# A decoder kernel on one Trainium2 core: gate layer and matrix powers made one unrolled stage

## The reference

```
g  = sigmoid(x @ Wg.T + bg)                # gate layer
u  = x * g                                 # gated input
h_t = A_c h_(t-1) + B_c u_t,  y_t = C_c h_t + D_c u_t      # for each channel c
```

## Time and profile before

| | |
|---|---|
| median of 3 runs | 5916.88 us (5911.08 to 5918.68) |
| profiled execution | 5911.98 us, span 5910.1 us |
| mean granted TensorE clock | 0.839 |
| PE busy | 4607.9 us, 78% |
| DVE / ACT / POOL busy | 3770.6 / 1886.1 / 2643.7 us |
| DMA | 625.22 MB, mean 106 GB/s |

### The profile page before, as it was taken

The page is one execution under the profiler, slowest core; times in us unless marked ns, Lnnn a source line. Parts: engine busy times, 40 slices in busy tenths (PEclk is TensorE's granted clock), DMA queues, the critical chain, the costliest instruction groups (busy, mean ns, idle before and its releaser), DMA issues. The chain is left out here.

```text
span 5910.1 us, 44058 instructions
## 1 busy us (share of the span) xinstructions
PE 4607.9 (78%) x13049; PEld 2461.4 (42%) x13057; DVE 3770.6 (64%) x3977; ACT 1886.1 (32%) x2769; POOL 2643.7 (45%) x1515
## 2 busy tenths in 40 slices
PE   7799796563999970997882887777777869968887
PEld 3699775442444420443330333333333323434443
DVE  2233342656224668554884999999999977744555
ACT  1111111111223446112773444334443334413332
POOL 0344452220001224010887899999999963311110
PEclk9555798555999985999886999989999989979998
DMA  1100112212223669452445115114142124510000
GB/s 64 63 0 0 41 57 84 89 54 87 93 96 139 224 240 374 152 189 88 172 167 209 56 59 174 60 65 160 58 147 72 60 107 163 202 66 22 28 28 22
DMA packets 314169, 625.22 MB, mean 106 GB/s; under 512 B 34407, under 2 KB 101896, under 8 KB 301204
## 3 DMA queue, kind: packets, MB, share of 16 engines
q1 hardware_dynamic: 295956, 589.74, 28.4%
q10 hardware_dynamic: 18048, 33.56, 1.5%
HBM read 404.48 MB, written 218.73 MB: 105 GB/s over the span
## 5 line engine op out<-in xcount | busy, mean ns | idle before, releaser
L1945 PE MATMUL sc_yp<-sc_Z,sc_idn 128*128 128x512 f32 x2048 | 1079.5, 664 | 425.1 <-POOL sc_Z L1875 216.9
L1869 POOL TENSOR_TENSOR sc_X<-sc_Bm,sc_w 128x1024 f32<-128x1024 f32 x512 | 1188.6, 2353 | 13.3 <-issue 12.5
L1945 PEld LDWEIGHTS sc_yp<-sc_Z,sc_idn 128*128 128x128 f32 x2048 | 411.5, 210 | 1053.3 <-issue 650.0
L1891 ACT ACTIVATE sc_A<-sc_dt,keep_A 128x1024 f32<-128x1024 f32 x512 | 572.1, 1117 | 526.6 <-DVE sc_Z L1981 427.0
L1110 PE MATMUL ff_ps<-ffn_R 128*128 128x512 f32 x1536 | 667.6, 595 | 7.8 <-ACT ff_o L1146 6.7
L1130 PE MATMUL ff_ps<-ffn_downT,ffn_R 128*128 128x512 f32 x768 | 332.8, 596 | 193.0 <-DVE ffn_R L1303 193.0
L1981 DVE TENSOR_TENSOR sc_Z<-sc_A,sc_Cm 128x1024 f32<-128x1024 f32 x384 | 470.1, 1224 | 17.6 <-issue 4.4
L1976 DVE TENSOR_TENSOR_SCAN sc_A<-sc_A,sc_hc,sc_X 128x1024 f32<-128x1024 f32 x192 | 450.2, 2345 | 0.0
L1110 PEld LDWEIGHTS ff_ps<-ffn_R 128*128 128x128 f32 x1536 | 290.3, 190 | 379.6 <-issue 352.1
L1976 DVE TENSOR_TENSOR_SCAN sc_A<-sc_A,sc_X 128x1024 f32<-128x1024 f32 x192 | 438.2, 2282 | 14.8 <-POOL sc_X L1869 14.8
L1875 POOL TENSOR_TENSOR sc_Z<-sc_H,sc_Cm 128x1024 f32<-128x1024 f32 x128 | 300.1, 2344 | 149.8 <-DVE sc_H L1976 149.8
(11 more groups left out here) (348 smaller groups left out, 7509.1 us busy)
## 6 DMA issues: line engine op xcount, KB each, us to landing
sc_Bm<-d_xd SPq DMA_DIRECT2D x64, 512.0 KB, 12.2
sc_Cm<-d_xd SPq DMA_DIRECT2D x64, 512.0 KB, 14.5
ffn_gate_d<-ff_o SPq DMA_DIRECT2D x96, 256.0 KB, 2.3
ff_g<-ffn_gate_d SPq DMA_DIRECT2D x24, 1024.0 KB, 6.0
ffn_up_d<-ff_o SPq DMA_DIRECT2D x96, 256.0 KB, 6.2
ffn_g_d<-ff_z SPq DMA_DIRECT2D x24, 1024.0 KB, 6.4
ffn_R<-ffn_g_d SPq DMA_DIRECT2D x24, 1024.0 KB, 7.2
ffn_R<-ffn_up_d SPq DMA_DIRECT2D x24, 1024.0 KB, 9.4
```

Source lines behind the costliest of these rows:

```text
L1869: nc.gpsimd.tensor_tensor(X[:, k % RX], Bm[:, n], w[:, j % 2], ALU.mult).then_inc(db, 1)
L1891: nc.scalar.activation(A[:, k % 2], dt[:, j % 2], ACT.Exp, scale=keepA[:, n:n + 1]).then_inc(ex, 1)
L1945: last = nc.tensor.matmul(yp[:, e * TB:(e + 1) * TB], idn[:], Z[:, k % RZ, e * TB:(e + 1) * TB], start=(n == 0), stop=(n == NS - 1))
```

## The change

`gate_stage` and `powers_stage` become `gate_powers_stage`. All loops are unrolled; the order of work is one list `STEPS` of (round i, m, u), 160 of them. There are 32 gate tiles (8 blocks x 4 slices) of four matmuls, and five steps to a tile: in the first four of each five steps TensorE does one gate matmul ahead of the step's own. Sigmoids go behind each fifth step on ScalarE, products behind the eviction of each fifth step on VectorE. The sigmoid is written in place in PSUM. The h matmuls move from the end of a round to m = 6, from an own buffer `cbd` that GpSimd fills at m = 5. The B rows are now taken out by VectorE too. A and C come packed in one array, and m = 0 uses it directly. The two PSUM tiles of the powers share one bank for each unit. The store of `xg` stands at the end of SP's program.

```diff
-def powers_stage(nc, a_pk, b_pk, c_pk, dp_pk, e0, mask, ident, keep, hp_d):
+def gate_powers_stage(nc, x_t, wg_t, bg, xgp, ac_pk, b_pk, dp_pk, e0, mask, ident, keep, hp_d):
+    STEPS = [(i, m, u) for i in range(NI) for m in range(SQ) for u in range(NS)]
+    TILES = T // NT * KD
+    EVERY = len(STEPS) // TILES
+    HM = 6
...
+        pg = s.ps("pg", [P, KD, NT])
+        pp = s.ps("pp", [P, NS, 512])
...
         @block.sync
+            for t, v in ((acin, ac_pk), (bin_, b_pk), (msk, mask), (idn, ident), (e0s, e0), (dp, dp_pk)):
                 sp.dma_start(t[:], v).then_inc(cst, 16)
+            sp.dma_start(w[:], wg_t.rearrange("(k p) e -> p k e", p=P)).then_inc(w_in, 16)
+            sp.dma_start(bias[:], bg).then_inc(w_in, 16)
+            for nb in range(T // NT):
+                if nb >= 2:
+                    sp.wait_ge(prod, 1 + (nb - 1) * KD)
+                sp.dma_start(x[:, nb % 2], x_v[:, :, nb * NT:(nb + 1) * NT]).then_inc(x_in[nb % 2], 16)
...
             sp.wait_ge(h_te, 2)
             sp.dma_start(hp_d[:, TAU:2 * TAU]..., ht[:]...).then_inc(out_d, 16)
+            sp.wait_ge(prod, 1 + TILES)
+            for k in range(KD):
+                sp.dma_start(xgp...[k], xg[:, k]).then_inc(stored, 16)
             sp.wait_ge(out_d, 33)
+            sp.wait_ge(stored, 1 + 16 * KD)
...
         @block.gpsimd
+            for i, m, u in STEPS:
+                if m == 0:
+                    pool.wait_ge(t_bd[u], 1 + i * SQ)
+                    pool.wait_ge(sq[u], 1 + max(i * SQ - SQ + 4, 0))
+                    expand(nc.gpsimd, pbd[:, u], acin[:, groups(i, u), 0:16], msk[:]).then_inc(p_bd[u], 1)
+                else:
+                    pool.wait_ge(ev[u], evicted(i, m - 1))
+                    expand(nc.gpsimd, pbd[:, u], r2[:, u, :, 0:16], msk[:]).then_inc(p_bd[u], 1)
+                if m == HM - 1:
+                    pool.wait_ge(h_mm[u], 1 + i)
+                    expand(nc.gpsimd, cbd[:, u], r2[:, u, :, 16:32], msk[:]).then_inc(c_bd[u], 1)
...
         @block.tensor
+            def gate_part(r):
+                t, k = r // KD, r % KD
+                nb, e = t // KD, t % KD
+                if r == 0:
+                    pe.wait_ge(w_in, 33)
+                if t >= KD:
+                    pe.wait_ge(prod, 1 + t - KD + 1)
+                pe.wait_ge(x_in[nb % 2], 1 + nb // 2 * 16 + 16)
+                last = nc.tensor.matmul(pg[:, e], w[:, k, e * P:(e + 1) * P], x[:, nb % 2, k], start=(k == 0), stop=(k == KD - 1))
+                if k == KD - 1:
+                    last.then_inc(mm, 1)
+            for c, (i, m, u) in enumerate(STEPS):
+                n = 2 ** m if m < 4 else 0
+                if c % EVERY < KD:
+                    gate_part(c // EVERY * KD + c % EVERY)
+                pe.wait_ge(t_bd[u], 1 + i * SQ + m + 1)
+                if m:
+                    pe.wait_ge(ev[u], evicted(i, m - 1))
...
+                if m == HM:
                     pe.wait_ge(c_bd[u], 1 + i + 1)
                     for g in range(GB):
+                        last = nc.tensor.matmul(ps1[:, u, g, 8:9], cbd[:, u, g], r1[:, u, g, 15:16], start=True, stop=True)
                     last.then_inc(h_mm[u], 1)
...
         @block.scalar
+            for c, (i, m, u) in enumerate(STEPS):
...
+                if c % EVERY == EVERY - 1:
+                    t = c // EVERY
+                    act.wait_ge(mm, 1 + t + 1)
+                    nc.scalar.activation(pg[:, t % KD], pg[:, t % KD], ACT.Sigmoid, bias=bias[:, t % KD:t % KD + 1]).then_inc(gated, 1)
...
         @block.vector
+            for c, (i, m, u) in enumerate(STEPS):
+                if c >= NS:
+                    evict(*STEPS[c - NS])
+                    if (c - NS) % EVERY == 0 and c - NS >= EVERY:
+                        product((c - NS) // EVERY - 1)
+                turn(i, m, u)
+            for c in range(len(STEPS) - NS, len(STEPS)):
+                evict(*STEPS[c])
+            product(TILES - 1)
```

More of the change, by code:

```diff
@@ L61, in sem @@
         return self.sems[-1]
[L64 to L129, removed]
@@ L154, in powers_stage @@
         tbd = s.sb("tbd", [P, NS, GB, P])
+        cbd = s.sb("cbd", [P, NS, GB, P])
         h, ht = s.sb("h", [P, G]), s.sb("ht", [G, P])
[L156 to L159, removed]
+        pg = s.ps("pg", [P, KD, NT])
+        pp = s.ps("pp", [P, NS, 512])
@@ L160, in powers_stage @@
+        ps1 = pp[:, :, 0:4 * 16].rearrange("p u (g n) -> p u g n", g=GB)
+        ps2 = pp[:, :, 64:64 + 4 * 64].rearrange("p u (g n) -> p u g n", g=GB)
+        cst, zset, out_d, h_tr, h_te, h_ok = [s.sem(n) for n in ("cst", "zset", "out_d", "h_tr", "h_te", "h_ok")]
+        w_in, x_in = s.sem("w_in"), [s.sem("x_in0"), s.sem("x_in1")]
+        mm, gated, prod, stored = s.sem("mm"), s.sem("gated"), s.sem("prod"), s.sem("stored")
+        init, p_bd, t_bd, sq, ev, kept, c_bd, h_mm = [
             [s.sem(f"{n}{u}") for u in range(NS)] for n in
-            ("init", "p_bd", "t_bd", "sq", "ev1", "ev2", "kept", "c_bd", "h_mm", "h_ok")]
+            ("init", "p_bd", "t_bd", "sq", "ev", "kept", "c_bd", "h_mm")]
@@ L181, in _ @@
             nc.gpsimd.memset(zero[:], 0.0).then_inc(zset, 1)
[L182 to L195, removed]
+            pool.wait_ge(cst, 1 + 16 * 6)
@@ L197, in _ @@
         @block.tensor
         def _(pe):
[L199 to L217, removed]
+            pe.wait_ge(cst, 1 + 16 * 6)
@@ L218, in _ @@
+            for c, (i, m, u) in enumerate(STEPS):
[5 more added lines that the diff above has]
+                    pe.wait_ge(ev[u], evicted(i, m - 1))
+                if m == 1:
+                    pe.wait_ge(init[u], 1 + i * 2 + 2)
+                if m == HM:
                     pe.wait_ge(c_bd[u], 1 + i + 1)
                     for g in range(GB):
-                        last = nc.tensor.matmul(ps1[:, u, g, 64:65], pbd[:, u, g], r1[:, u, g, 15:16], start=True, stop=True)
+                        last = nc.tensor.matmul(ps1[:, u, g, 8:9], cbd[:, u, g], r1[:, u, g, 15:16], start=True, stop=True)
@@ L221, in _ @@
                     last.then_inc(h_mm[u], 1)
-            for u in range(NS):
-                pe.wait_ge(h_ok[u], 1 + HB // NS)
-            nc.tensor.transpose(ps2[0:G, 0, 0], h[:], idn[:]).then_inc(h_tr, 1)
+                for g in range(GB):
+                    gg = (i * NS + u) * GB + g
+                    if n:
+                        nc.tensor.matmul(ps1[:, u, g, 0:n], pbd[:, u, g], r1[:, u, g, 16 - n:16] if m else bin_[:, gg:gg + 1],
+                                         start=True, stop=True)
+                    cols = 16 + max(n, int(m == 4))
+                    last = nc.tensor.matmul(ps2[:, u, g, 0:cols], tbd[:, u, g], r2[:, u, g, 0:cols] if m else acin[:, gg, 0:cols],
+                                            start=True, stop=True)
@@ L226, in _ @@
+                last.then_inc(sq[u], 1)
+            pe.wait_ge(h_ok, 1 + HB)
+            pe.wait_ge(prod, 1 + TILES)
+            nc.tensor.transpose(pg[0:G, 0, 0:P], h[:], idn[:]).then_inc(h_tr, 1)
         @block.scalar
         def _(act):
[L228 to L231, removed]
-                for u in range(NS):
-                    act.wait_ge(h_mm[u], 1 + i)
-                    act.wait_ge(kept[u], 1 + i * (LV + 2))
-                    act.sem_inc(seen)
-                    nc.scalar.copy(r2[:, u, :, 0:16], ain[:, groups(u)]).then_inc(init[u], 1)
-                    nc.scalar.copy(r1[:, u, :, 15], bin_[:, groups(u)]).then_inc(init[u], 1)
-                    nc.scalar.copy(r2[:, u, :, 16], cin[:, groups(u)]).then_inc(init[u], 1)
-                    act.wait_ge(init[u], 1 + i * 4 + 3)
-                    nc.scalar.copy(keep["bk"][:, groups(u), 15], bin_[:, groups(u)]).then_inc(init[u], 1)
-                for m in range(SQ):
-                    for u in range(NS):
-                        n = 2 ** m if m < 4 else 0
-                        if n:
-                            act.wait_ge(sq[u], 1 + i * SQ + m + 1)
-                            nc.scalar.copy(r1[:, u, :, 16 - 2 * n:16 - n], ps1[:, u, :, 0:n]).then_inc(ev1[u], 1)
-                        if m >= 3:
-                            act.wait_ge(ev2[u], 1 + i * E2 + written(m + 1))
-                            act.sem_inc(seen)
-                            nc.scalar.copy(keep["pw"][:, m - 3, groups(u)], r2[:, u, :, 0:16]).then_inc(kept[u], 1)
-                        if m == 4:
-                            act.wait_ge(ev1[u], 1 + i * 4 + 4)
-                            nc.scalar.copy(keep["bk"][:, groups(u), 0:15], r1[:, u, :, 0:15]).then_inc(kept[u], 1)
-                            nc.scalar.copy(keep["ck"][:, groups(u)], r2[:, u, :, 17:33]).then_inc(kept[u], 1)
@@ new lines, in _ @@
+            act.wait_ge(cst, 1 + 16 * 6)
+            act.wait_ge(w_in, 33)
+            for c, (i, m, u) in enumerate(STEPS):
+                if m == 0:
+                    act.wait_ge(sq[u], 1 + i * SQ)
+                    act.wait_ge(kept[u], 1 + i * KEPT)
```

(37 more changed lines are left out.)

58 lines of the change are left out of this document (24 added, 34 removed).

## The result

The changed kernel takes 5949.7 us (5947.09 to 5951.04, 4 runs) against 5916.0 for the kernel before (5911.08 to 5918.68, 4 runs): ratio 1.0057, 95% interval 1.004 to 1.0075. Slower, by 33.7 us; the forecast was 5950.

The account below looks back on a forecast made before the run. TensorE at the lower clock bounds the merged stage: 13.5 + 409.7 + 218.4 + 3.9 + 21.1 + 3.4 = 670.0 us to the state-space stage against 636.5, so 5916.9 + 33.5 = 5950 us; range 5895 to 5985.

Parts of the forecast that it names:

- The clock, the step that decided the sign: Merged stage: single wide matmuls among small passes leave TensorE at 1.2 GHz; wide passes cost 218 us instead of 110.
- Rival 2: Merged stage at the upper clock throughout, since a busy TensorE gets it: 227 us sooner, 5690 us; chance 0.09.
- Rivals 1 and 4: Merged stage partly at upper clock: 1, steps m>=4 only, 5880 us, chance 0.10; 4, even within 12 us, 0.03.
- TensorE's work: Merged stage at the lower clock: 1,920 small passes, 409.7 us, plus 256 wide gate passes, 218.4 us.
- Loads cancel as charged: Merged stage: a wide pair's first weight load is seen, the following small pass's load hidden; no load charged.
- rival 3: Merged stage: wide passes' weight loads not hidden among small ones, 27 us more (5978) or 55 us (6005); chance 0.05.
- Chain, sigmoids, products, reloads of x hidden: Merged stage: eviction-expansion-transpose chain (2.13 us a step for m >= 4), gate's elementwise work and x reloads cost nothing behind TensorE.
- The wait of VectorE that I named as a sign: Merged stage's profile: VectorE's long wait at the evictions, for TensorE, not at the transposes, for POOL.
- Start: Merged stage's first gate matmul moves from 10.25 to 13.5 us, +3.3 us for six constant loads; bounds 12 and 16.
- Boundary and store: Merged stage's end: one 5 us boundary goes; 3.9 us tail, 21.1 us unhidden gated-input store, then 3.4 us boundary.
- The closing tally: Summary after the sum: 30 us gaps, 23 us x waits, 14 us start and boundary saved; 108 us paid for wide passes.

Follow-up runs that it names:

- pairs: The changed kernel with the gate's matmuls two and two, at the first and third of each five steps: 5851.6 us, ratio 0.9894 to the kernel before.
- tiles: The changed kernel with all four matmuls of a gate tile at the first of each five steps: 5796.2 us, ratio 0.9807 to the kernel before.
- blocks: The changed kernel with sixteen gate matmuls in one go ahead of each twentieth step: 5835.1 us, ratio 0.9875 to the kernel before.

## Why the prediction was right

- *The clock, the step that decided the sign:* right. The stage ran at 1.2 GHz; but the sign I named for it, a granted clock of 0.50 in the table, was wrong, since the column read 1.00. The pace of the passes is the evidence, and the pairs, tiles and blocks confirm it. My reason held as far as it went: with the same work, wide matmuls in groups bring the clock up and single ones don't. It isn't the whole condition, since with enough extra matmuls around them single ones ran at the upper level too (1.00 from 20.7 to 416.6 us). Rival 2's premise, a busy TensorE gets the full clock, fell with the version of 223 extra matmuls: busy 735.6 of 736 us at 0.50. Rivals 1 and 4 needed part of the stage at the upper level; TensorE's 628.2 us are the whole work at the lower one, so there was none.
- *TensorE's work*, 409.7 + 218.4 = 628.1 us: measured 628.2 us busy in 629. Loads cancel as charged (rival 3 fell).
- *Chain, sigmoids, products, reloads of x hidden:* right; TensorE waits for nothing after 16.1 us. The wait of VectorE that I named as a sign is only partly as I said: 283 us at the evictions, but still 160 at the transposes.
- *Start:* 13.5 us forecast (12 to 16), measured 16.06. The term is mis-sized by 2.6 us: I priced the loads ahead of the gate's (3.3 us; they cost 2.9) and left out that the merged stage increments 45 semaphores before its barrier, now ahead of the whole kernel: 2.9 us more than the gate's 8.
- *Boundary and store:* the tail, from the end of the last small pass at 644.27 to the end of hp's issue at 647.89, was 3.6 us instead of 3.9, the store 3.3 + 18.0 us, 0.2 more than taken. The first transfer came at 672.7 instead of 670.0, nearly all of it by the start.
- *The closing tally* (30, 23 and 14 us taken away, 108 paid) gives 41 us, not the 33.5 of the sum. It sets the gate's passes before at 110 us, where the rows have TensorE busy 119.9 us at a mean clock of 0.93, and leaves the later start out. The forecast doesn't rest on it.
- *The number:* 5950 forecast, 5949.7 measured. That it fits to less than 1 us is luck. The first transfer moved by 36.1 us where 33.5 were forecast, and the spans differ by 38.7 us where the medians differ by 33.7.
- *Rival 2's price*, a stage at the full clock, 5690 us without a word on what keeps it up: reached in part, at 5741 with 365 extra matmuls and the store early. Steps of m >= 4 stand at 2.13 us as worked out there; those of m < 4 cost 3.30 us instead of 2.40, since the extra matmuls make TensorE their bound.

## What to carry to other kernels

When two stages are merged so that wide matmuls are strewn among small ones, price the wide ones at the lower clock: they may cost twice what they cost back to back, and the overlap must pay for that first. Putting four of them in a row turned a loss of 34 us into a gain of 117 us with the same work. Read the clock from the spacing of passes wherever no change of level has been recorded yet, and look at what a moved store had behind it: in this kernel moving it under the last steps gave 20.5 us up to the next stage, and 24 us of the whole time.

## What the runs showed of the hardware

- TensorE busy all the time isn't enough for the upper clock: 735.6 of 736 us at 0.50 with 223 extra matmuls, beside 393.6 of 395 us at 1.00 with 318, one more of 192 columns in part of the steps. More work made the kernel 305 us faster.
- The clock's column can show 1.00 over 629 us of passes at 1.2 GHz (0.85 us for a wide one), where the trace holds no change of level yet.
- Small passes with a weight load each take 0.2134 us at the lower level and 0.11 at the upper, though they are 1 to 24 columns wide. The load follows the clock too: one that stands by itself is recorded with 0.34 us at the lower level and 0.19 at the upper.
- A stage's start costs 0.08 us for each semaphore that it has and increments ahead of its barrier (36 more in the kernel before: first transfer at 4.44 instead of 1.62 us). That it is the increment that takes the time is read from the kernel's text, not measured apart.
